# Feed-forward weights sized in the first sizing pass and turned beside the output projection

## The chip, the cores and the metric

One core of one Trainium2 chip runs the whole decoder layer as one program. The metric is the device time of that program in microseconds (us). TensorE (PE) multiplies, VectorE (DVE), ScalarE (ACT) and GpSimd (POOL) work elementwise, SyncE (SP) issues most DMAs. All of them run their own instruction streams and meet only at semaphores.

## What is computed

The layer is self-attention with 8-bit fake quantisation, cross-attention, and a feed-forward network, each with a residual and a layer norm behind it. Eight batches of 512 tokens of width 512. What matters for this change is the last part, and the projection in front of it:

```python
def fake_quant_weight(w, bits=8):
    scale = jnp.max(jnp.abs(w)) / 127
    return jnp.clip(jnp.round(w / scale), -128, 127) * scale
def qat_lora_linear(x, W, b, A, B):
    base = einsum('bsi,oi->bso', x, fake_quant_weight(W)) + b
    return base + 2 * einsum('bsr,or->bso', einsum('bsi,ri->bsr', x, A), B)
x = layernorm(x + (attended @ Wo + bo))             # x2 below
h = gelu(qat_lora_linear(x, W_fc, b_fc, A_fc, B_fc))      # W_fc: 2048 x 512
x = layernorm(x + qat_lora_linear(h, W_proj, b_proj, A_proj, B_proj))  # W_proj: 512 x 2048
```

The scale of each feed-forward weight is a maximum over the whole tensor, so no element can be quantised before all have been seen once. The ranks A and B are 16 wide. TensorE needs the weights with the contracted index on the partitions, so both weights and all four rank matrices are turned (transposed) through TensorE and PSUM.

## The kernel before

The program is a row of stages. All five engines meet at a barrier between stages: `barrier` (L218) drains an engine, adds one to `phase_end` and waits until all five have done so; `STAGES` lists them. Each stage streams the eight batches through scratch tensors in HBM. `arena` is one on-chip buffer carved anew for each stage, and `bank` is PSUM, eight banks of 128 x 512 f32. The stages that matter, in order:

- **First sizing pass** (up to barrier 3): `qkv_size` (TensorE, L845 and L850) computes the QKV product in pairs of banks only to find its largest value; `size_qkv` (VectorE, amax at L1398) reduces each pair. Twelve pairs per batch, four pairs fit in PSUM (`qkv_red` starts at 4). In the middle of a batch VectorE quantises the next one's input (`quantise_h`, L1565 and L1569). SP's queue stores that input and loads one two batches ahead (L437, L433).
- **Score rows** (up to barrier 6): ends with VectorE waiting for ScalarE's last sums (L1260) in `keep_rows`.
- **Cross-attention** (up to barrier 10): 32 groups of four heads. TensorE does L997, L1005, L1013 and L1041; VectorE reduces and clips (L1785, L1811). The last group's values are stored by SP (L597).
- **Output projection** (barrier 10 to 11): `project_out` (L1092) does 32 units of four f32 matmuls (each is two records in the trace), one bank per unit, eight banks in turn. VectorE's `second_norm` adds the bias (L1866), adds a bank to the residual (L1870), takes statistics (L1455), does a Newton square root (L1461 to L1472) and scales (L1480). SP stores the result, x2, to scratch and loads the next inputs (L675, L632, L629). ScalarE only issues the DMAs of the two weights (L1359), 4 MB each.
- **Weights** (barrier 11 to 12): for W_fc and then W_proj VectorE takes the maximum over 128 x 8192 (L1398), GpSimd reduces over partitions (L736), VectorE makes the scale, the int8 weight (L1918), the f16 weight (L1920), and spreads B (L1925). TensorE turns four 128 x 128 pieces into a bank (L1111), VectorE moves each bank out (L1896, and L1907 with L1908 for the A matrices, which are kept as an f16 and a remainder), and makes the remainder of B (L1947, L1950).
- **Feed-forward** (barrier 12 to 13): x2 of batch 0 is loaded back (L710), turned by TensorE (`turn_x2`, L1142), moved by ScalarE (L1369), split by VectorE (`split_x2`, L1959 and L1960), and `ranks` (L1149) multiplies it with A. Then `ffn` runs 16 slices per batch (L1162, L1165, L1173 to L1176) with ScalarE's Gelu (L1376) and VectorE's split (L1986, L1987). The norm of a batch is done in slices 1 to 3 of the next (`third_norm`).

The order of work on each engine is the order of the program; no planner is used.

## Time and profile before

| | us |
|---|---|
| three runs | 3144.04, 3149.09, 3150.22 (median 3149.09) |
| the profiled execution | 3145.82 |
| its span, first to last instruction | 3144.0 |
| TensorE / VectorE / ScalarE busy | 2659.6 / 2504.7 / 1443.7 |
| mean granted TensorE clock | 0.895 of full |

The page divides the span into 40 slices of 78.6 us. A digit is the busy share of the slice in tenths; `PEclk` is the clock that TensorE was granted, in tenths of 2.4 GHz, so 5 is 1.2 GHz. The profiled execution lies 3.3 us below the median of the runs.

### The profile page before, as it was taken

The numbers are of one execution on the slowest core, as the hardware profiler recorded it, in microseconds if no ns is written. First come the engines' busy times: TensorE is split into PE (matmuls) and PEld (weight loads), VectorE is DVE, ScalarE is ACT, GpSimd is POOL, SyncE is SP. The second block draws the span as 40 slices with busy tenths as digits, with TensorE's granted clock in tenths as the row PEclk, the third lists the DMA queues.
The fourth block names the chain that finished last, engine by engine and source line by source line (L and its number), as shares of the span: only waits on it lengthen the run. The fifth ranks groups of instructions, "written<-read, shape, count | busy, mean of one in ns | idle before, by whom it ended". The sixth has DMA issues, their size and how long they took to land. (4 is left out here: it accounts for less than half of the span.)

```text
span 3144.0 us, 44439 instructions
## 1 busy us (share of the span) xinstructions
PE 2659.6 (85%) x13112; PEld 1034.6 (33%) x13160; DVE 2504.7 (80%) x4278; ACT 1443.7 (46%) x2366; POOL 159.0 (5%) x147
## 2 busy tenths in 40 slices
PE   7999999967777747777769699999999379999997
PEld 4444432211111124444335222222224234444443
DVE  5988679999998979999888688888868854444454
ACT  3320043318999989999423255555530011211111
POOL 0000043310000000000000000111100000000000
PEclk9999999975555569999989899999999679999999
DMA  8561122214333333333125433434356200000000
GB/s 314 167 224 64 40 97 94 93 80 141 127 120 122 111 103 116 104 116 104 57 71 184 114 106 99 115 98 116 114 182 248 69 27 27 28 27 27 27 27 27
DMA packets 196495, 324.41 MB, mean 103 GB/s; under 512 B 32281, under 2 KB 118297, under 8 KB 187025
## 3 DMA queue, kind: packets, MB, share of 16 engines
q1 hardware_dynamic: 192160, 306.12, 30.0%
q10 hardware_dynamic: 4208, 16.78, 1.4%
q8 instruction: 58, 0.95, 0.1%
q14 instruction: 69, 0.56, 0.1%
HBM read 192.32 MB, written 130.51 MB: 103 GB/s over the span
## 5 line engine op out<-in xcount | busy, mean ns | idle before, releaser
L1398 DVE TENSOR_REDUCE stats<-bank 128x1024 f32 (+1 forms) x352 | 408.0, 1217 | 60.5 <-PE bank L845 28.1
L1260 ACT ACTIVATE arena<-arena,scale 128x512 bf16<-128x512 int8 x512 | 408.1, 799 | 53.4 <-DVE arena L1638 53.4
L905 PE MATMUL bank<-arena 64*128 64x512 bf16 x512 | 306.4, 605 | 104.9 <-DVE arena L1631 66.9
L1278 ACT ACTIVATE arena<-arena,scale 128x512 f32<-128x512 int8 x512 | 370.5, 803 | 13.1 <-DMA arena<-dq_scr 11.0
L1631 DVE CUSTOM_DVE_ANT_0 arena<-bank,arena,fac 128x512 int8<-128x512 f32 x512 | 349.8, 747 | 23.2 <-PE bank L905 10.2
L1785 DVE TENSOR_REDUCE arena<-bank 128x2 f32<-128x1024 f32 x256 | 312.5, 1223 | 54.7 <-PE bank L997 38.8
L1342 ACT ACTIVATE arena<-bank 128x1024 f32<-128x1024 f32 x256 | 248.0, 1022 | 189.4 <-PE bank L1013 189.4
L1376 ACT ACTIVATE arena<-bank,arena,fac 128x512 f32<-128x512 f32 x128 | 99.5, 777 | 458.8 <-PE bank L1165 458.8
L1041 PE MATMUL bank<-arena 128*32 128x512 f32 x2048 | 270.9, 606 | 0.0
L1248 ACT ACTIVATE arena<-bank,floor_c,fac 128x1024 int8<-128x1024 f32 x96 | 115.6, 1205 | 337.8 <-PE bank L845 287.2
L1986 DVE TENSOR_SCALAR arena<-arena 128x512 f16<-128x512 f32 x128 | 54.7, 428 | 260.7 <-ACT arena L1376 260.7
L845 PE MATMUL bank<-arena 128*128 128x512 bf16 x989 | 239.9, 382 | 11.3 <-DMA arena<-hq_scr 7.4
L1173 PE MATMUL bank<-arena 128*128 128x512 f16 x1024 | 242.0, 379 | 3.6 <-DVE arena L1987 3.2
L1162 PE MATMUL bank<-arena 128*128 128x512 f16 x1024 | 241.9, 379 | 0.0
L922 PE MATMUL bank<-identb,arena 128*128 128x128 bf16 x2048 | 138.8, 222 | 115.1 <-DVE arena L1684 115.1
L997 PE MATMUL bank<-arena 128*128 128x512 f16 x512 | 156.4, 389 | 25.1 <-DMA arena<-half_scr 13.0
L1811 DVE TENSOR_SCALAR arena<-arena 128x1024 f32<-128x1024 f32 (+1 forms) x192 | 168.2, 876 | 8.3 <-ACT arena L1342 8.3
L922 PEld LDWEIGHTS bank<-identb,arena 128*128 128x128 bf16 x2048 | 116.7, 99 | 176.6 <-DVE arena L1684 133.9
L1684 DVE TENSOR_SCALAR arena<-arena,inv 128x2048 bf16<-128x2048 f32 x128 | 163.5, 1277 | 10.8 <-ACT arena L1278 10.8
L905 PEld LDWEIGHTS bank<-arena 64*128 64x128 bf16 x512 | 51.7, 101 | 359.6 <-DVE arena L1631 349.4
L1665 DVE TENSOR_SCALAR arena<-bank 128x2048 bf16<-128x2048 bf16 x128 | 155.8, 1217 | 0.0
L1005 PE MATMUL bank<-arena 128*128 128x512 f16 x512 | 153.6, 383 | 0.0
(202 smaller groups left out, 3477.5 us busy)
## 6 DMA issues: line engine op xcount, KB each, us to landing
dq_scr<-arena SPq DMA_DIRECT2D x128, 256.0 KB, 2.0
arena<-dq_scr SPq DMA_DIRECT2D x128, 256.0 KB, 2.7
arena<-half_scr SPq DMA_DIRECT2D x256, 128.0 KB, 2.8
qkv_scr<-arena SPq DMA_DIRECT2D x8, 3072.0 KB, 9.7
arena<-in_x SPq DMA_DIRECT2D x16, 1024.0 KB, 8.4
half_scr<-arena SPq DMA_DIRECT2D x32, 512.0 KB, 4.1
arena<-qkv_scr SPq DMA_DIRECT2D x128, 128.0 KB, 2.2
x_scr<-arena SPq DMA_DIRECT2D x16, 1024.0 KB, 4.5
```

The lines of the kernel that those rows point to most:

```text
L845: last = mm(dst, wqkv_q[:, k, P * u:P * u + P], hq[:, k, :], start=k == 0, stop=k == KC - 1)
L905: return mm(dst, qE[r, h // 2, P * t:P * t + P], kE[r, h // 2, :], start=True, stop=True)
L922: last = nc.tensor.transpose(PT[s % 2][:, j, P * t:P * t + P], aG[:, s % 2, t, P * j:P * j + P], identb[:, :])
L1041: last = mm(bank[XD * g:XD * g + XD, 7 if k < 2 else 6, :], w, eT[:, par, g, c, :], start=c == 0, stop=c == NT - 1)
L1162: mm(dst, Wf[:, k, P * s:P * s + P], xx[:, par, k, :], start=k == 0 and n == 0, stop=False)
L1173: mm(bank[:, t, :], gg[:, f % 3, P * t:P * t + P], Wp[:, f, :], start=f == 0 and n == 0, stop=False)
L1260: last = A(e_dump[:, NT * (h % 2) + t, :], dq8[:, h % 4, t, :], ACT.Exp, bias=negm_b[:, par, c:c + 1], scale=scale[:, S_DOTS:S_DOTS + 1], ...
L1278: A(eG[:, s % 2, t, :], dqG[:, s % 4, t, :], ACT.Exp, bias=negm_g[:, par, c:c + 1], scale=scale[:, S_DOTS:S_DOTS + 1]).then_inc(S("eG_done ...
L1342: A(eT[:, r % 2, 2 * a:2 * a + 2, c, :], bank[:, 2 + 2 * a:4 + 2 * a, :], ACT.Exp, scale=XSCALE / HALF ** 2).then_inc(S("eX_done"), 1)
L1398: return V.tensor_reduce(dst, src, ax, ALU.max, apply_absolute_value=True)
L1631: V.tensor_tensor_reduce(dq8[:, s, t, :], bank[:, 4 * (h % 2) + t, :], floor_row, fac[:, C_DOTS:C_DOTS + 1], -3.0e38, ALU.add, ALU.max, ac ...
L1785: V.tensor_reduce(mxX[:, mp, hs, 2 * u:2 * u + 2], bank[:, at:at + 2, :], AX.X, ALU.max).then_inc(S("sX_red"), 1)
```

## The change

- **Sizing.** Both weights are read once more, in eight parts of 1 MB (128 x 2048 f32), during the first sizing pass. SP issues `load_part(0)` behind the first store of that pass and `load_part(b + 1)` behind `load_h(b + 2)`, each after a wait for the part before. VectorE reduces part b to `w_peak` behind pair 2 of batch b. The reduction to two peaks, GpSimd's reduction over partitions and four small scale steps go into the score-row stage.
- **Ranks.** The 16 DMAs of A and the two of B are issued by SP at the start of cross-attention; VectorE spreads B (`spread_ranks`, 16 instructions without a wait between them) in the last group.
- **Quantising.** ScalarE loads W_fc in four quarters behind its last cross-attention copy, makes it int8 in four passes of 128 x 2048 (`quantise_weight`), loads W_proj over it, widens W_fc to f16 in four passes (`widen_weight`), quantises W_proj, moves ten B copies, widens W_proj, and moves 32 weight banks.
- **Turning.** The projection uses banks 0 to 4 in turn and turns go to banks 5 to 7. TensorE turns the ten rank banks behind units 4 to 13, 16 banks of W_fc behind units 14 to 21, 16 of W_proj behind 22 to 29, and the first x2 behind 30 and 31. VectorE moves the five A banks in `halves_of_a` and subtracts the B halves in `halves_of_b` behind batch 4.
- **Barriers and order.** The diff takes 10, 11 and 12 out of `STAGES` and out of all engines. The norm of the last projected batch moves into slices 1 to 3 of the first feed-forward batch. SP's load of x2 for batch 0 now stands ahead of the last two stores of x2. The bias DMAs stand behind a wait for unit 3.
- Semaphore names `y_peak` and `o8_done` are replaced by ones in use; this changes no instruction's place.

```diff
-STAGES = (3, 5, 6, 7, 8, 9, 10, 11, 12, 13)
+STAGES = (3, 5, 6, 7, 8, 9, 13)
@@ first sizing pass, SP and VectorE
             for b in range(NB):
                 store_hq(b)
+                if b == 0:
+                    load_part(0)
                 if b + 2 < NB:
                     load_h(b + 2)
+                if b + 1 < NB:
+                    sp.wait_ge(S("part_in"), 16 * b + 16)
+                    load_part(b + 1)
...
+                    if u == 2:
+                        dve.wait_ge(S("part_in"), b * 16 + 16)
+                        amax(w_peak[:, bass.ds(b, 1)], part).then_inc(S("part_sized"), 1)
@@ cross-attention, SP and VectorE
+            for r in range(P // R):
+                sp.dma_start(arep_f[R * r:R * r + R, :], A_fc).then_inc(S("ranks_in"), 16)
+                sp.dma_start(arep_p[R * r:R * r + R, :], A_proj).then_inc(S("ranks_in"), 16)
...
+                        if last and (c, u) == (1, 0):
+                            spread_ranks()
@@ output projection, TensorE
-                    pe.wait_ge(S("wo_evac"), b * NT + t + 1)
+                if u >= 5:
+                    pe.wait_ge(S("wo_evac"), u - 4)
...
+            for u in range(NB * NT):
+                project_out(u // NT, u % NT)
+                if u == 4:
+                    pe.wait_ge(S("sumS_done"), GROUPS)
+                    pe.wait_ge(S("oX_evac"), GROUPS)
+                if 4 <= u < 14:
+                    turn_ranks(u - 4)
+                for n in (2 * u, 2 * u + 1):
+                    if 28 <= n < 44:
+                        turn_fc(n - 28)
+                    if 44 <= n < 60:
+                        turn_proj(n - 44)
+                    if 60 <= n:
+                        turn_first_x2(n - 60)
@@ output projection, ScalarE
+            for q in range(KC):
+                load_weight(wn[...], chunk(W_fc)[...], q)
+            quantise_weight(0, S_WFC)
+            for q in range(KC):
+                act.wait_ge(S("w8_done"), q + 1)
+                load_weight(wn[...], chunk(W_proj)[:, q, :], q)
+            widen_weight(wnh)
+            quantise_weight(1, S_WPROJ)
+            for n in range(5):
+                moved_by_act(half, 5 + n)
+                moved_by_act(full, 5 + n).then_inc(S("w_moved_act"), 1)
+            act.wait_ge(S("w8_done"), 8)
+            widen_weight(wnp)
+            for n in range(FC):
+                moved_by_act(Wf[...], 10 + n, True).then_inc(S("w_moved_act"), 1)
+            for n in range(FC):
+                moved_by_act(Wp[:, n, :], 26 + n, True).then_inc(S("w_moved_act"), 1)
@@ output projection, VectorE
+            for b in range(NB - 1):
+                ch = add_projected(b)
+                for k in range(3):
+                    second_norm(ch, b, k)
+                ch.end()
+                if b == 4:
+                    halves_of_b()
+            add_projected(NB - 1)
```

A turn beyond the third waits for the move of the turn three before it (`MOVED_BY`): five moves by VectorE, then 37 by ScalarE, then ScalarE's copies of x2.

## Rows read from the trace of the kernel before

**Rows 1.** The page: granted TensorE clock by slice of 78.6 us.
```profile
PEclk9999999975555569999989899999999679999999
```
**Rows 2.** TensorE's waits, 2330 to 2560 us: waiter, cause, total, times, longest.
```profile
PE bank L1111 <- DVE arena L1920: 58.2, 2, 31.4
PE bank L1142 <- DMA arena<-x_scr: 9.9, 1, 9.9
PE bank L1092 <- POOLq L220: 6.2, 1, 6.2
```
**Rows 3.** Timeline, 2296 to 2360 us: start, duration, instruction, idle before it.
```profile
2326.56 7.93 PE L1041 MATMUL bank<-arena 128*32 128x512 f32 x72
...
2340.72 19.82 PE L1092 MATMUL bank<-arena 128*128 128x512 f32 x39 [6.23 <-POOLq L220]
```
**Rows 4.** Timeline, 2536 to 2610 us: the first x2, the first ranks, a later x2.
```profile
2550.41 0.43 DVE L1959 CAST arena<-arena 128x512 f16<-128x512 f32 x1 [0.65 <-ACT arena L1369]
2550.87 0.69 DVE L1960 TENSOR_TENSOR arena<-arena 128x512 f16<-128x512 f32 x1
...
2551.62 3.38 PE L1149 MATMUL bank<-arena 128*128 128x512 f16 x8 [1.88 <-DVE arena L1960]
...
2585.78 0.60 PE L1142 MATMUL bank<-ident,arena 128*128 128x128 f32 x4
...
2586.21 1.89 PE L1162 MATMUL bank<-arena 128*128 128x512 f16 x8
```
**Rows 5.** Busy time by stretch: length, PE, PEld, DVE, ACT, POOL, PEclk, DMA share, GB/s.
```profile
2341.00:2344.00 3.00, 3.00 (x4) 1.23 (x5) 2.12 (x4) 0.00 (x0) 0.00 (x0) 0.50 0.76 206
...
2352.00:2400.00 48.00, 48.00 (x113) 21.22 (x112) 37.06 (x99) 0.00 (x0) 0.00 (x0) 1.00 0.73 282
...
2520.00:2532.00 12.00, 8.34 (x76) 8.08 (x77) 11.56 (x26) 0.00 (x0) 0.00 (x0) 0.55 0.00 0
```
**Rows 6.** Groups by line and shape, 2462 to 2538 us: busy, mean ns, idle before.
```profile
L1398 DVE TENSOR_REDUCE peak<-arena 128x1 f32<-128x8192 f32 x2 | 17.4, 8686 | 4.0 <-ACTq L220 4.0
L1918 DVE TENSOR_SCALAR arena<-arena,fac 128x8192 int8<-128x8192 f32 x2 | 9.0, 4486 | 0.1
L1950 DVE TENSOR_TENSOR arena<-arena 32x2048 f16<-32x2048 f32 x2 | 4.6, 2284 | 0.1
...
L1907 DVE TENSOR_SCALAR arena<-bank 128x512 f16<-128x512 f32 x5 | 3.4, 683 | 0.0
```
**Rows 7.** Timeline of the weights stage: turns of f16 pieces, four to a bank.
```profile
2525.55 5.30 PE L1111 MATMUL bank<-identh,arena 128*128 128x128 f16 x48 [0.87 <-DVE arena L1896]
```
**Rows 8.** ScalarE by size: groups of the page, one of 150 to 400 us.
```profile
L1278 ACT ACTIVATE arena<-arena,scale 128x512 f32<-128x512 int8 x512 | 370.5, 803 | 13.1 <-DMA arena<-dq_scr 11.0
L1376 ACT ACTIVATE arena<-bank,arena,fac 128x512 f32<-128x512 f32 x128 | 99.5, 777 | 458.8 <-PE bank L1165 458.8
L1248 ACT ACTIVATE arena<-bank,floor_c,fac 128x1024 int8<-128x1024 f32 x6 | 7.2, 1206 | 180.1 <-PE bank L845 180.1
```
**Rows 9.** Groups by line and shape, 2352 to 2452 us: VectorE's cycle of a batch.
```profile
L1870 DVE TENSOR_TENSOR arena<-bank,arena 128x512 f32<-128x512 f32 x29 | 18.7, 687 | 13.6 <-PE bank L1092 12.6
```
**Rows 10.** Timeline of the first sizing pass, 196 to 262 us.
```profile
216.75 0.96 SPq L437 DMA_DIRECT2D hq_scr<-arena  x1
...
219.21 1.23 DVE L1398 TENSOR_REDUCE stats<-bank 128x1 f32<-128x1024 f32 x1 [0.50 <-PE bank L845]
...
227.26 1.27 DVE L1565 TENSOR_SCALAR arena<-arena,inv 128x2048 int8<-128x2048 f32 x1
```
**Rows 11.** Groups, 150 to 400 us: a reduction of a whole 128x2048 tile.
```profile
L1398 DVE TENSOR_REDUCE stats<-arena 128x1 f32<-128x2048 f32 x3 | 6.8, 2281 | 0.3 <-ACT arena L1208 0.3
```
**Rows 12.** DMA issues, 2330 to 2400 us: KB each, us to landing.
```profile
arena<-in_L_ffn_W_fc ACTq DMA_DIRECT2D x1, 4096.0 KB, 15.0
```
**Rows 13.** Timeline, 1120 to 1140 us: VectorE at the end of the score rows.
```profile
1128.75 0.20 DVE L1619 COPY neg_m<-arena 128x64 f32<-128x64 f32 x1 [9.29 <-ACT arena L1260]
```
**Rows 14.** Timeline, 2296 to 2350 us: VectorE in the last cross-attention group.
```profile
2322.41 1.23 DVE L1811 TENSOR_SCALAR arena<-arena 128x2048 f32<-128x2048 f32 x1 [2.52 <-ACT arena L1342]
```

More of the change, by code:

```diff
@@ L683, in after_batch @@
                 load_x1(b + 2, par)
+            sp.wait_ge(S("wo_mm"), NT)
+            with nc.allow_non_contiguous_dma(reason="a column of 2048 numbers"):
+                sp.dma_start(bf_s[:, :], col(b_fc)).then_inc(const_in, 16)
+            sp.dma_start(bp_s, b_proj.rearrange("(a n) -> a n", a=1).broadcast_to([P, D])).then_inc(const_in, 16)
             with sp.Fori(0, NB // 2 - 1) as j:
@@ new lines, in project_out @@
+            def project_out(b, t):
+                u = b * NT + t
+                if t == 0:
+                    pe.wait_ge(S(f"oK_in{b % 2}"), 16 * (b // 2) + 16)
+                if u >= 5:
+                    pe.wait_ge(S("wo_evac"), u - 4)
+                for o in range(KC):
+                    last = mm(bank[:, u % 5, :], oK[:, b % 2, o, P * t:P * t + P], Wo_s[:, o, :],
+                              start=o == 0, stop=o == KC - 1)
+                last.then_inc(S("wo_mm"), 1)
+            turned = [0]
@@ new lines, in weight_bank, with turn_f32 @@
+            def weight_bank():
+                n = turned[0]
+                turned[0] += 1
+                if n >= 3:
+                    engine, count = MOVED_BY[n - 3]
+                    pe.wait_ge(S(engine), count)
+                return bank[:, 5 + n % 3, :]
+            def turn_f32(parts):
+                dst = weight_bank()
+                for q, src in enumerate(parts):
+                    last = nc.tensor.transpose(dst[:, P * q:P * q + P], src, ident[:, :])
+                last.then_inc(S("w_turned"), 1)
@@ new lines, in widen_weight, with moved_by_act @@
+            def widen_weight(dst):
+                for q in range(4):
+                    r = slice(QW * q, QW * q + QW)
+                    A(dst[:, r], wn8[:, r], ACT.Copy).then_inc(S("wnh_ready"), 1)
+            def moved_by_act(dst, n, f16=False):
+                act.wait_ge(S("w_turned"), n + 1)
+                src = bank[:, 5 + n % 3, :]
+                return A(dst, src.bitcast(F16)[:, 0:512] if f16 else src, ACT.Copy)
+            for q in range(KC):
+                load_weight(wn[:, QW * q:QW * q + QW].rearrange("p (a d) -> p a d", d=D), chunk(W_fc)[:, KC * q:KC * q + KC, :], q)
@@ L1873, in second_norm @@
-                norm_stats(ch, xK[:, par])
-                for t in range(NT):
-                    last = normed(xK[:, par, t, :], xK[:, par, t, :], t)
-                last.then_inc(S("x2_ready"), 1)
-                ch.end()
-            batches(dve, second_norm)
-            barrier(dve, 11)
-            pair = ((S_WFC, C_FC, B_FCS, 9), (S_WPROJ, C_PROJ, B_PROJS, 10))
-            moved = [0]
-            def move(dst, src_rows=slice(0, P), cast=None, scale_by=None):
-                n = moved[0]
-                moved[0] += 1
-                dve.wait_ge(S("w_turned"), n + 1)
-                src = bank[src_rows, n % 4, :]
-                if cast:
-                    src = src.bitcast(F16)[:, 0:512]
-                if len(dst.shape) == 3:
-                    src = src.rearrange("p (a b) -> p a b", b=P)
-                if scale_by is None:
-                    return V.tensor_copy(dst, src)
-                return V.tensor_scalar(dst, src, scale_by, None, ALU.mult)
@@ new lines, in add_projected, with second_norm @@
+                    if 4 <= u < 9:
+                        halves_of_a(u - 4)
+                return ch
+            def second_norm(ch, b, k):
+                par = b % 2
+                if k == 0:
+                    dve.wait_ge(S("wo_evac"), b * NT + NT)
+                    norm_moments(ch, xK[:, par])
+                if k == 1:
+                    norm_factors(ch)
+                if k == 2:
+                    for t in range(NT):
+                        last = normed(xK[:, par, t, :], xK[:, par, t, :], t)
+                    last.then_inc(S("x2_ready"), 1)
```

296 lines of the change are left out of this document (144 added, 152 removed).

## The prediction

> **What bounds the kernel now.** I read the slices first, then TensorE's waits, then the timeline around them. The granted clock falls to 7 and 9 tenths in two neighbouring slices near the end [rows 1]; these slices hold the weights stage. TensorE's waits there name the reason: 58.2 us in two waits for VectorE's f16 weight, 9.9 us for the first x2 to come back, 6.2 us at the barrier behind cross-attention [rows 2]. The timeline gives the two ends. The last cross-attention matmul ends at 2334.5 us (2326.56 + 7.93) and the first matmul of `ranks` starts at 2551.6 [rows 3, 4]. Everything that the change moves at the end of the kernel lies in these 217.1 us. In them TensorE needs its time only for the projection: inside a full-clock stretch one record takes 48/112 = 0.43 us [rows 5] (113 are listed, one cut at the edge), so 256 records need 109.7 us. The rest, 107 us, is barriers, half clock and VectorE's serial chain on the weights. Behind it the feed-forward is all TensorE, and in front of it cross-attention isn't touched. So the question is how much of 107 us comes back.
>
> **The new path, part by part.** I lay out TensorE's stream from 2334.5 us on.
>
> - *Barrier behind cross-attention gone.* Its 6.2 us [rows 2] go. TensorE's own conditions (output of the reductions, the first inputs) are long met; banks 0 to 3 were read before the last clip. Because TensorE doesn't pause, the half clock behind the pause goes too: 39 records took 19.8 us where 39 x 0.43 is 16.7 [rows 3], and the row from 2341 shows 0.50 [rows 5]. Both are contained in counting the projection at 109.7 us straight from 2334.5.
> - *Turns of ranks.* Ten banks of f32. A bank costs TensorE 0.43 us at full clock: a turned x2 bank starts at 2585.78 and the next work at 2586.21 [rows 4]. 10 x 0.43 = 4.3 us.
> - *Turns of weights.* 32 banks of f16. In the weights stage 48 pieces, twelve banks, took 5.3 us [rows 7], 0.44 us a bank, at a clock of about 0.55 [rows 5]. At 1.2 GHz that is 0.44, at 2.4 GHz half of it. Bounds 7 and 14 us; I take 7, since the stretch from 2352 to 2400 shows 1.00 with nothing but this matmul [rows 5] and the turns add to TensorE's work. These are 6.7 us at 0.21.
> - *First x2.* Two of its four banks behind unit 30: 0.9 us. The other two lie in the drain below.
> - *Waits for the moves.* A turn waits for the move three before it. ScalarE moves the last B bank just behind unit 13, two copies of at most 0.78 us [rows 8], and then widens W_proj, four passes of 128 x 2048, before the first W_fc bank can be moved. The trace has no pass of that size. ScalarE's rows give 0.78 us for 512 and 1.21 for 1024 elements, 0.84 ns an element [rows 8], so 2.07 us for 2048. From above it can't exceed four passes of 512 with an SBUF source, 4 x 0.80 = 3.2 us [rows 8]. With 2.07 the first W_fc bank is free 1.5 + 8.3 + 0.7 = 10.5 us behind unit 13, while TensorE wants it after two units and three turns, 7.5 us. Stall 3.0 us; 7.5 with 3.2 us a pass; none if the passes start early. I take 3.0, from the rows with a like size step. Later turns come two to a unit of 3.43 us and find their banks moved.
> - *PSUM.* The projection has five banks instead of eight. VectorE needs 13.7 - 1.9 = 11.8 us a batch (13.6 us idle over 29 adds, four to a batch) [rows 9]. From the add of a batch's last bank to the first of the next lie about 11 us, with the B halves (2 x 2.3 us and two small ones, some 6 us [rows 6]) 17 us. The unit that reuses that bank starts five units and their turns later, over 18 us. No stall, margin 1 to 2 us. The A halves (0.68 + 0.42 us each, five [rows 6]) fall in batches 1 and 2, where the ten rank turns give VectorE 0.43 us a unit more; it ends 1 us behind and catches up.
> - *DMAs.* W_fc landed 15.0 us after its issue while W_proj was in flight beside it [rows 12]. Now W_fc goes at 2335, W_proj at about 2352, behind the fourth int8 pass; widening W_fc covers its landing. W_proj is int8 by about 2370, and the first B bank is turned at 2371. SP issues the two bias DMAs ahead of the inputs of batch 2, which then leave at 2351 for use at 2364; an input of this size is in flight with W_proj, 5 MB at the stretch's 282 GB/s [rows 5], so at the worst 18 us if all of W_proj went first. I cost it at nothing, and 5 us if it did.
> - *The drain.* Behind unit 31 VectorE adds the last bank (0.2 + 0.69 us [rows 9]), then splits four pieces of x2, 0.43 + 0.69 us each with no wait on ScalarE any more [rows 4], 4.6 us with gaps; then `ranks`. 5.6 us. The norm of batch 7 is no longer here. It goes beside slices 1 to 3 of the first feed-forward batch, where the norm of the batch before stands in every other batch.
>
> Sum: 109.7 + 4.3 + 6.7 + 0.9 + 3.0 + 5.6 = 130.2 us against 217.1, a gain of 86.9 us. I leave `ranks` at its old 3.38 us (half clock [rows 4]), since TensorE idles nearly 5 us ahead of it and 6.2 us of idle was enough for 0.50 [rows 3, 5].
>
> *What is paid elsewhere.* (1) First sizing pass: a pair costs TensorE 1.73 us and VectorE 1.23 with 0.50 idle [rows 10]. Twelve pairs leave 6 us, `quantise_h` takes 2.5 of them (1.27 and a like cast [rows 10]); the new reduction takes 2.28 [rows 11]. So it fits: the lag behind pair 2 is mostly made up before `quantise_h` and never reaches 3.9 us, what four pairs in PSUM allow. Batch 0 is different. Its part is issued at 217.7 behind the store [rows 10], and VectorE wants it at 220.4. I take 8 us to land, half of what 4 MB beside another 4 MB took [rows 12]: 1 MB, but behind stores and a load in the same queue. Landing at 225.6 makes pair 3 free at 229.1 instead of by 226.1: 3.0 us (0 for a landing before 222.5, 6 for 228.5). If VectorE's new work hid behind nothing it would be 8 x 2.28 = 18.3 us. (2) Score rows: one tiny reduction in front, 0.3 us; the four scale steps at the end stand before a copy that waited 9.29 us for ScalarE [rows 13]: nothing. (3) Spreading B: 16 small instructions, about 5 us, ahead of two clips that waited 2.5 and 1.9 us in the last group [rows 14], with more idle behind; I cost it at 0, at most 1. (4) 18 DMA issues at the start of cross-attention: SP there waits for the end of group 0 anyway: 0.
>
> 3145.8 - 86.9 + 3.0 + 0.3 = 3062.2 us. The profiled execution lies 3.3 us below the median of runs, which spread over 6 us; I add nothing for that.
>
> *A rule that speaks against the change.* VectorE made an int8 weight at 4486/8192 = 0.55 ns an element [rows 6], ScalarE's rows give 0.84 [rows 8]. The Trainium skill (ScalarE: Activation LUTs, Rules for kernel authors) says to use VectorE and not ScalarE for such plain arithmetic, VectorE being up to about three times faster an element. The trace agrees in direction, at 1.5 times. By three times, a pass of 2048 would be about 3.4 us as an estimate from that page, the stall above some 8 us and the time about 3067.
>
> **The rivals.**
>
> *A. ScalarE sets the pace.* The 16 large passes cost 3.2 us each [rows 8]. For it: no such pass is in the trace, and ScalarE did nothing here before. Against: the step from 512 to 1024. Stall 7.5 instead of 3.0: 3066.7; with inputs of batch 2 late as well, 3072.
>
> *B. The reductions aren't hidden in the sizing pass.* For it: VectorE is TensorE's partner at every pair there. Against: it idles 0.50 us at each pair [rows 10]. 18.3 instead of 3.0 us: 3077.5.
>
> *C. The first x2 isn't early.* SP loads it behind a store and a load of batch 5; if it is only issued when unit 31 ends, the 9.9 us that TensorE waits for it now [rows 2] come back: 3072. Against: it should leave four units before it is wanted.
>
> *D. Clock and landing are kind.* TensorE keeps 2.4 GHz through the drain (`ranks` in 1.7 instead of 3.38 us), part 0 lands in time and ScalarE is early: 3062.2 - 1.7 - 3.0 - 3.0 = 3054.5.
>
> *E. Slower: half clock in the projection.* If the many waits on moves made TensorE's projection run at 1.2 GHz, its 121.6 us of work would take 243.2: 3184, slower. The gain of 83.6 is used up when 83.6/121.6, 69%, of that stretch is at half clock. For it: 0.50 follows a pause of 6.2 us [rows 3, 5]. Against: between full-clock matmuls of 3.43 us a unit there is one expected wait of 3 us in 125. The Trainium skill (TensorE: Matmul & The Clock Gate, A second HAM failure mode) describes a kernel whose cycling through PSUM banks let the clock swing between both levels; no row here shows it for such short gaps.
>
> *F. It doesn't do what it says*: a wait I have overlooked holds the turns until the projection is over. 42 banks at ScalarE's 0.78 us each plus the passes, some 45 us back: 3107.
>
> **How the numbers follow.** Forecast 0.66, A 0.13, B 0.07, C 0.02, D 0.08, E 0.02, F 0.02. The range runs from D's 3054, less 1, to B's 3077, plus 3: 3053 to 3080; it leaves out E, F and the tails. A measurement of this kernel can tell about 0.2%, 6.3 us, from no change. All cases but E are faster by more than that; I give faster 0.96, same 0.01, slower 0.03.
>
> **What the profile will show.** Right: TensorE passes from L1041's successor to the projection without a pause and at 1.00; one stall of 2 to 4 us behind unit 15, waiting for ScalarE; ScalarE's 2048 passes near 2.1 us; `ranks` about 130 us behind the last cross-attention matmul; sizing pass longer by 3 us in batch 0 and by nothing later; the feed-forward as long as now. Wrong: TensorE waits in several units for ScalarE or DMA, a PEclk under 0.9 in the projection, or a longer stretch between units 19 and 24, where VectorE subtracts the B halves.

## The result: 3063.8 us where 3062.2 was forecast

| | before | after |
|---|---|---|
| median of four runs, us | 3146.95 (3144.04 to 3150.22) | 3063.81 (3063.38 to 3064.36) |
| profiled execution / its span | 3145.82 / 3144.0 | 3064.36 / 3062.6 |
| TensorE / VectorE / ScalarE busy | 2659.6 / 2504.7 / 1443.7 | 2652.0 / 2462.7 / 1495.8 |
| granted TensorE clock | 0.895 | 0.905 |

After to before is 0.9736, 95% interval 0.9719 to 0.9752: 83 us less. The sum was 1.6 us off the median and 2.2 us off the profiled execution. That closeness is partly luck: the late inputs of batch 2 cost 4.2 us that the sum didn't have, while the stall for ScalarE was 1.7 us shorter and the stretch from `ranks` to the end 1.9 us shorter than in it. Line numbers have moved: the projection is now L1111, ranks L1200, the last cross-attention matmul L1057, the reductions (amax) L1486, the split of x2 L2031 and L2032.

The slices of the page of after, to be held against [rows 1]:

```profile
PE   7999989986777747777678889999999999999997
...
PEclk9999999995555559999988989999999999999999
```

The low slices at the weights stage are gone. Counted along the row they are slices 32 and 33 of [rows 1], at 6 and 7 tenths of full clock; the prediction read 7 and 9, which enters no sum. What TensorE still waits for between 2330 and 2500 us in after (waited for, us in total, times, longest), where [rows 2] had 58.2, 9.9 and 6.2:

```profile
PE bank L1200 <- DVE arena L2032: 4.2, 1, 4.2
PE bank L1111 <- DMA arena<-oT_scr: 2.4, 1, 2.4
PE bank L1135 <- ACT arena L1426: 1.3, 1, 1.3
```

The first is the drain, foreseen. The third is the stall for ScalarE, 1.3 us where I had 3.0. The second I had costed at nothing. TensorE's timeline of after shows all three in place (start us, us, engine, line, operands, count, idle before and what ended it), with the projection's first record right behind the last cross-attention record (2329.91 + 7.93):

```profile
2329.91 7.93 PE L1057 MATMUL bank<-arena 128*32 128x512 f32 x72
2337.78 4.56 PE L1111 MATMUL bank<-arena 128*128 128x512 f32 x10
...
2366.66 0.60 PE L1129 MATMUL bank<-ident,arena 128*128 128x128 f32 x4
2369.65 5.40 PE L1111 MATMUL bank<-arena 128*128 128x512 f32 x8 [2.39 <-DMA arena<-oT_scr]
...
2402.06 0.39 PE L1135 MATMUL bank<-identh,arena 128*128 128x128 f16 x4
2403.70 0.40 PE L1135 MATMUL bank<-identh,arena 128*128 128x128 f16 x4 [1.26 <-ACT arena L1426]
...
2458.59 0.61 PE L1135 MATMUL bank<-identh,arena 128*128 128x128 f16 x8
2459.04 3.65 PE L1111 MATMUL bank<-arena 128*128 128x512 f32 x8
2462.53 1.04 PE L1167 MATMUL bank<-ident,arena 128*128 128x128 f32 x8
2463.40 3.60 PE L1111 MATMUL bank<-arena 128*128 128x512 f32 x8
2466.84 1.04 PE L1167 MATMUL bank<-ident,arena 128*128 128x128 f32 x8
2472.12 2.72 PE L1200 MATMUL bank<-arena 128*128 128x512 f16 x8 [4.25 <-DVE arena L2032]
```

The stretch from the last cross-attention matmul to `ranks` is 2472.12 - 2337.78 = 134.3 us. It was 217.1 before, and 130.2 in the forecast.

**The whole account of the profiled execution.** Up to the end of cross-attention after is 3.3 us later (2337.8 against 2334.5; forecast 3.3). The projection stretch is 82.8 us shorter (forecast 86.9). From `ranks` to the end it takes 590.5 instead of 592.4 us (forecast: the same). Then 3.3 - 82.8 - 1.9 = -81.4, and 3145.8 - 81.4 = 3064.4, what was measured.

### The profile page after: what moved, and what is told of

It reads as the page before. It is cut to its first block, busy times and chain, and to the rows that moved or that the text cites. A ratio compares the mean times of both kernels' runs of the same rounds, so it can differ in the third digit from the quotient of the medians.

```text
span 3062.6 us, 44241 instructions
## 1 busy us (share of the span) xinstructions
PE 2652.0 (87%) x13112; PEld 1025.9 (33%) x13160; DVE 2462.7 (80%) x4238; ACT 1495.8 (49%) x2424; POOL 159.1 (5%) x146
## 4 chain that ended last, share of the span: by engine, by line
PE 50%; issue 30%; DVE 15%; ACT 2%; DMA 1%; DVEq 1%; SPq 0%; ACTq 0%; POOLq 0%; POOL 0%
PE bank L1057 8%; PE bank L1224 7%; PE bank L1213 7%; DVE stats L1486 6%; PE bank L1013 4%; PE bank L1021 4%; PE bank L997 4%; PE bank L1111 3%; DVE arena L1785 2%; PE bank L834 1%; PE bank L841 1%; PE bank L1029 1%; ACT arena L1329 1%; PE bank L972 1%; PE bank L861 1%
## 5 line engine op out<-in xcount | busy, mean ns | idle before, releaser
L1486 DVE TENSOR_REDUCE stats<-bank 128x1024 f32 (+1 forms) x352 | 405.9, 1215 | 44.1 <-PE bank L898 26.8
L1329 ACT ACTIVATE arena<-arena,scale 128x512 f32<-128x512 int8 x512 | 370.3, 802 | 13.3 <-DMA arena<-dq_scr 11.3
L1462 ACT ACTIVATE arena<-bank,bf_s,fac 128x512 f32<-128x512 f32 x128 | 99.5, 778 | 459.2 <-PE bank L1216 459.2
L1057 PE MATMUL bank<-arena 128*32 128x512 f32 x2048 | 270.1, 604 | 0.0
L861 PE MATMUL bank<-arena 128*128 128x512 bf16 x989 | 240.3, 383 | 14.3 <-DMA arena<-hq_scr 7.4
```

The source lines that it names most:

```text
L861: last = mm(dst, wqkv_q[:, k, P * u:P * u + P], hq[:, k, :], start=k == 0, stop=k == KC - 1)
L1057: last = mm(bank[XD * g:XD * g + XD, 7 if k < 2 else 6, :], w, eT[:, par, g, c, :], start=c == 0, stop=c == NT - 1)
L1329: A(eG[:, s % 2, t, :], dqG[:, s % 4, t, :], ACT.Exp, bias=negm_g[:, par, c:c + 1], scale=scale[:, S_DOTS:S_DOTS + 1]).then_inc(S("eG_done ...
L1486: return V.tensor_reduce(dst, src, ax, ALU.max, apply_absolute_value=True)
```

## The experiments

All ran in rounds beside the kernel before. Totals of one kernel spread over 1 to 7 us, so effects of a few us are read from local stretches of the traces, and totals only where they are larger. For all of them, T is the time from the start of the projection to the start of `ranks`.

| kernel | median, us | ratio to before, 95% | T, us | wait for batch 2's inputs, us |
|---|---|---|---|---|
| after | 3063.81 | 0.9736 (0.9719 to 0.9752) | 134.3 | 2.4, then half clock |
| after_again | 3065.22 | 0.9751 (0.9734 to 0.9767) | 132.7 | 2.4 |
| e_bias_late | 3062.01 | 0.9739 (0.9723 to 0.9755) | 130.0 | none |
| e_wproj_wait | 3060.90 | 0.9736 (0.9720 to 0.9753) | 130.0 | none |
| e_part0_early | 3061.22 | 0.9732 (0.9715 to 0.9748) | 134.4 | 2.4, then half clock |
| e_widen_early | 3063.63 | 0.9742 (0.9726 to 0.9759) | 130.8 | 2.0 |
| e_x2_late | 3063.83 | 0.9745 (0.9729 to 0.9762) | 132.2 | 2.2 |
| e_splits_all | 3059.15 | 0.9732 (0.9716 to 0.9748) | 128.8 | 2.2 |
| e_turns_twice | 3072.90 | 0.9772 (0.9756 to 0.9788) | 140.6 | 2.2, then half clock |
| e_barrier10 | 3068.01 | 0.9754 (0.9737 to 0.9770) | 133.1 | 0.6 |
| e_reduce_twice | 3067.05 | 0.9750 (0.9734 to 0.9766) | 136.2 | 2.9, then half clock |
| e_reduce_thrice | 3091.11 | 0.9828 (0.9812 to 0.9845) | 133.1 | 2.9 |
| e_best | 3047.55 | 0.9693 (0.9677 to 0.9710) | 124.9 | none |

after_again is the changed kernel once more. It ran beside the first three experiments; the local stretches of the others are held against it too.

> The changed kernel once more, unedited, as the yardstick on this chip for the three runs beside it. Both theories: 3063 to 3065 us, span about 3062.6, TensorE idle 2.4 us for the values of batch 2 and 2.85 us in the first sizing pass.

The 2.4 us wait came back, the half clock behind it didn't: the next eight records took 3.70 instead of 5.40 us. The granted clock of 2370 to 2374 us, first in after, then in after_again (stretch, length, busy us and count by engine, clock, DMA share, GB/s):

```profile
2370.00:2374.00 4.00, 4.00 (x7) 1.51 (x6) 3.37 (x17) 0.00 (x0) 0.00 (x0) 0.58 0.46 166
```

```profile
2370.00:2374.00 4.00, 4.00 (x13) 1.91 (x12) 3.31 (x18) 0.00 (x0) 0.00 (x0) 1.00 0.43 139
```

So 1.7 us of after's 134.3 differ between executions of one program.

### Why batch 2's inputs were late

In after SP issued two bias loads at 2351.87 and 2352.30, and the values of batch 2 at 2353.94. The bias of W_fc is a column of 2048 four-byte pieces. The four W_proj loads of 1 MB left ScalarE's queue at the same time. The line that loads the values, and their time to landing, in after:

```profile
L649 SPq DMA_DIRECT2D arena<-oT_scr x8: 383/392/441, 2278.4 to 2435.4; - x8
...
DMA to landing us min/median/max: 5.4/6.6/15.7
```

The median load lands in 6.6 us, this one in 15.7. Two edits separate the two neighbours. The first moves the bias loads behind the inputs of batches 2 to 7:

```diff
-            sp.dma_start(bf_s[:, :], col(b_fc)).then_inc(const_in, 16)
-            sp.dma_start(bp_s, b_proj.rearrange("(a n) -> a n", a=1).broadcast_to([P, D])).then_inc(const_in, 16)
             with sp.Fori(0, NB // 2 - 1) as j:
                 after_batch(j * 2, 0)
                 after_batch(j * 2 + 1, 1)
+            sp.dma_start(bf_s[:, :], col(b_fc)).then_inc(const_in, 16)
+            sp.dma_start(bp_s, b_proj.rearrange("(a n) -> a n", a=1).broadcast_to([P, D])).then_inc(const_in, 16)
```

> The two bias DMAs are issued behind the loop over the batches instead of ahead of it. Theory (the values of batch 2 come late because SP's queue first issues and moves the biases, 2048 pieces of 4 bytes and a broadcast): they leave 2 us earlier and land before unit 8; the wait of 2.4 us and the half clock behind it (8 records in 5.4 instead of 3.6 us) go, 4.2 us less than the unedited kernel, about 3059.8. Rival (the 4 MB of W_proj in flight at once are what slows them): they leave 2 us earlier and land at most 2 us earlier, 0 to 2 us less, and the half clock may stay.

The wait is gone and T is 130.0 us. The values landed 13.6 us after their issue, 1.2 us before TensorE came for them. The second edit leaves the biases and holds ScalarE's four loads of W_proj until the values are in:

```diff
+            act.wait_ge(S("oK_in0"), 32)
             for q in range(KC):
                 act.wait_ge(S("w8_done"), q + 1)
                 load_weight(wn[:, QW * q:QW * q + QW], chunk(W_proj)[:, q, :], q)
```

> ScalarE waits for the values of batch 2 to have landed before it issues the four loads of W_proj; the biases stay where they are. Theory of the bias DMAs: the values land hardly earlier, no change beyond 1 us. Rival (W_proj's traffic): the values land at about 2361 instead of 2369.6, the 2.4 us wait and the half clock go, 4.2 us less; W_proj is then int8 at about 2379 instead of 2370, still before ScalarE is wanted for the B banks, so nothing is given back. About 3059.8.

The values landed in 6.2 us, ScalarE stood 8.0 us for them, the wait of TensorE is gone, and T is again 130.0 us. The issues of this kernel and their landing show the biases freed as well: 3.0 us for `bf_s`, where after had 11.3, and 4.3 for `bp_s`, where after had 14.3 (what is loaded, queue, count, KB, us to landing).

```profile
arena<-in_L_ffn_b_proj SPq DMA_DIRECT2D x1, 256.0 KB, 4.3
...
bf_s<-in_L_ffn_b_fc SPq DMA_DIRECT2D x1, 8.0 KB, 3.0
```

It isn't the 2048 pieces that hold the values up, though. In e_x2_late and e_turns_twice, which leave both biases and W_proj as in after, `bf_s` landed in 3.0 us too, and the values still took 15.6. How late `bf_s` lands goes with its lead over the first load of W_proj: 3.0 us at leads of 0.77 and 0.68 us, 6.2 to 7.1 at 0.63 and 0.62, 11.3 to 13.5 at 0.55 to 0.51 (after, after_again, e_part0_early), while the values took 15.3 to 15.9 in all seven.

So the wait needs both: W_proj's 4 MB are the larger part (15.7 to 6.2). The two biases together are some 3.6 us: without them the values leave some 1.5 us earlier, counted from the start of the projection, and fly 2.1 us less. Which of the two biases matters, no run separates. Either edit is enough to end the wait. Both edits leave T at 130.0 us: everything in my sum but this one term adds up to the 130.2 I had, in part because the f16 turns (1.4 us over) and the stall for ScalarE (1.7 under) cancel. T falls by 2.7 us against after_again; the totals fall by 3.2 and 4.3, no more than their spread.

### The first part of W_fc

```diff
                         load_h(n)
+                    sp.dma_start(w_parts[:, 0, :], W_fc.rearrange("(p a) d -> p (a d)", p=P)[:, 0:KC * D]
+                                 ).then_inc(S("part_in"), 16)
                 sp.wait_ge(S("v_ready"), b * NT + NT)
...
-                if b == 0:
-                    load_part(0)
```

> Part 0 of W_fc is loaded behind the first two loads of the quantised input's source, some 18 us earlier. Theory (the only price of the sizing pass is VectorE waiting 5.0 us for part 0, of which TensorE's four pairs of banks hide all but 2.85): those 2.85 us go and every later part stays hidden, about 3061. Rival (the reduction itself costs, wherever its data is): TensorE still waits in the sizing pass, less than 1 us gained. Third: the load now collides with the input load that VectorE waits 6.6 us for, and 1 to 3 us are lost there instead.

The timeline of after, at the place of [rows 10]: VectorE stands 5.02 us for the part, and TensorE in its turn 2.85 us for VectorE. First VectorE, then TensorE:

```profile
225.41 2.29 DVE L1486 TENSOR_REDUCE w_peak<-arena 128x1 f32<-128x2048 f32 x1 [5.02 <-DMA arena<-in_L_ffn_W_fc]
227.62 4.61 DVE L1486 TENSOR_REDUCE stats<-bank 128x1 f32<-128x1024 f32 x4
```

```profile
214.00 12.03 PE L861 MATMUL bank<-arena 128*128 128x512 bf16 x54 [1.40 <-ACT arena L1280]
228.89 1.90 PE L861 MATMUL bank<-arena 128*128 128x512 bf16 x8 [2.85 <-DVE stats L1486]
```

With the load ahead of the wait both waits are gone. L866 of batch 0 starts at 227.55 us, where the kernel before has 227.64 and after 230.63, and the projection starts at 2335.0, where the eight kernels with this stretch unedited and no barrier in front start at 2337.0 to 2339.6. The term of 3.0 us is shown, and so is its cause. What the wait costs later varies: in seven of the other kernels half clock follows it.

### How much of VectorE is free in the sizing pass

Rival B said the reductions would not hide. In after they do: eight batches of the first sizing pass follow each other at 20.7 us as before (L866 starts at 230.63, 251.42, ... 375.74; in the kernel before at 227.64, 248.36, ... 372.68). Reducing each part twice (one added line) or three times (both) finds the edge.

```diff
+                        amax(tmpf[:, 6:7], part)
+                        amax(tmpf[:, 7:8], part)
                         amax(w_peak[:, bass.ds(b, 1)], part).then_inc(S("part_sized"), 1)
```

> In the first sizing pass VectorE reduces each part of W_fc twice (2.2 us more a batch), to measure how much of VectorE's time is really free there. Worked out: a batch costs TensorE 20.7 us (12 pairs of 1.73), VectorE 12 x 1.16 + 2.19 + 2.5 = 18.6 us back to back, so 2.1 us are free. Theory (the free time decides, four pairs in PSUM even it out): the second reduction just about fits, 0 to 4 us for the eight batches, all in all, beside the 2.2 us that batch 0 pays, since its part lands late: total 2 to 6 us up. Rival (lags behind a pair aren't made up before the quantising and each batch pays): 2.2 x 8 = 17 us.

> The same with each part reduced three times (4.4 us more a batch). Theory: VectorE then needs 23.0 us a batch against TensorE's 20.7 and sets the pace: 2.3 us for each of eight batches, 18 us, and some 2 us for batch 0: total 15 to 22 us up, and the free time comes out as 4.4 us less the lengthening of a batch. Rival (every reduction is paid in full): 35 us. Rival (the free time is larger than worked out): under 10 us.

Twice: 147.5 us from the first to the eighth L866 instead of 145.1. Of these 2.4 us 1.0 lies in the first batch, which still has half clock behind its wait (32 records in 8.00 us, 7.14 in after), and 0.2 to 0.3 in each other one, without a wait of TensorE. Its one large wait, in batch 0, is 5.0 instead of 2.9 us. The total is in the 2 to 6 us of the theory; the projection starts at 2343.7, 4 to 7 us later than elsewhere. Three times: TensorE waits for VectorE in every batch, and the seven batches take 166.7 us, 3.1 a batch where 2.3 was expected; the total is up by some 26 us, above the 15 to 22 I gave. TensorE's waits in the first sizing pass of e_reduce_thrice:

```profile
PE bank L861 <- DVE stats L1486: 22.9, 8, 7.7
```

Of them 7.7 us are batch 0's, and the other seven are 2.1 to 2.2 us each, as the theory has it. The size was off because of what follows the wait. TensorE's timeline, two batches in a row:

```profile
280.30 1.90 PE L861 MATMUL bank<-arena 128*128 128x512 bf16 x8 [2.22 <-DVE stats L1486]
282.04 7.14 PE L866 MATMUL bank<-arena 128*128 128x512 bf16 x32
...
303.49 3.29 PE L861 MATMUL bank<-arena 128*128 128x512 bf16 x8 [2.22 <-DVE stats L1486]
306.57 7.41 PE L866 MATMUL bank<-arena 128*128 128x512 bf16 x32
```

In four of the seven batches the eight records behind the wait take 1.90 us and the batch is 23.0 to 23.5 us long. In the other three they take 3.3 to 3.5 us (granted clock 0.57 from 303.4 to 306.6 us, 1.00 from 328.3 to 330.0) and the batch is 24.5 to 24.7. So the lengthening is 2.5 us a batch at full clock, and half clock in three batches adds 4.3 us in all. Batch 0 adds 5.2 (its L866 starts at 235.84, in after at 230.63) where some 2 were expected. VectorE itself still stands now and then, 6.9 us in all from 240 to 400 us, in the pairs ahead of each burst:

```profile
317.57 1.23 DVE L1486 TENSOR_REDUCE stats<-bank 128x1024 f32 x1 [0.50 <-PE bank L861]
319.29 1.22 DVE L1486 TENSOR_REDUCE stats<-bank 128x1024 f32 x1 [0.50 <-PE bank L861]
320.44 4.47 DVE L1486 TENSOR_REDUCE tmpf<-arena 128x1 f32 x2
324.82 2.28 DVE L1486 TENSOR_REDUCE w_peak<-arena  x1
```

So 4.4 - 2.5 = 1.9 us a batch are free, where 2.1 had been worked out, and the second reduction takes 2.2 of them for 0.2 to 0.3. The change's own 2.2 us a batch is hidden in full, with some 2 us of room behind it.

### What a turn costs

```diff
                 dst = weight_bank().bitcast(F16)
                 for q, src in enumerate(parts):
+                    nc.tensor.transpose(dst[:, P * q:P * q + P], src, identh[:, :])
+                for q, src in enumerate(parts):
                     last = nc.tensor.transpose(dst[:, P * q:P * q + P], src, identh[:, :])
```

> Each of the 32 f16 weight banks is turned twice by TensorE (the same four transposes again into the same bank), so that their cost appears a second time. Theory (turns lie on TensorE's path at their full price and the moves behind them are hidden): a unit with two turns goes from 3.93 to 4.35 to 4.45 us, the stretch from the last cross-attention matmul to ranks from 134.3 to 141 to 142.5 us, the total 7 to 8 us up. Rival 1 (turns hide under the weight loads or in waits for ScalarE): under 2 us. Rival 2 (ScalarE or VectorE sets the pace of these units, and turns only wait): under 2 us and TensorE's waits for ScalarE shrink instead.

In after a unit with two f16 banks takes 3.93 us, with them 0.45 and the unit 3.49, since the matmuls behind a turn run 3.65 instead of 3.60 us:

```profile
2434.98 0.61 PE L1135 MATMUL bank<-identh,arena 128*128 128x128 f16 x8
2435.43 3.65 PE L1111 MATMUL bank<-arena 128*128 128x512 f32 x8
2438.91 0.61 PE L1135 MATMUL bank<-identh,arena 128*128 128x128 f16 x8
```

Doubled (L1135 and the new L1137), a unit takes 4.38 us, 2430.57 to 2434.95:

```profile
2430.57 0.39 PE L1135 MATMUL bank<-identh,arena 128*128 128x128 f16 x4
2430.79 0.39 PE L1137 MATMUL bank<-identh,arena 128*128 128x128 f16 x4
2431.01 0.39 PE L1135 MATMUL bank<-identh,arena 128*128 128x128 f16 x4
2431.24 0.39 PE L1137 MATMUL bank<-identh,arena 128*128 128x128 f16 x4
2431.46 3.65 PE L1111 MATMUL bank<-arena 128*128 128x512 f32 x8
2434.95 0.39 PE L1135 MATMUL bank<-identh,arena 128*128 128x128 f16 x4
```

That is 0.22 us a bank, on the path in full: T is 140.6, and less the 1.6 us of half clock that this execution has and after_again doesn't (5.34 for 3.70), 138.9. Against after_again's 132.7 it is 6.3 us, plus 0.7 that the stall for ScalarE shrank (1.3 to 0.6) and 0.2 that the input wait did: 7.2 for 32 banks. The total is up by some 8 us over after_again. Rival F, turns that wait, would have shown waits for ScalarE at every unit; there is one.

### ScalarE's order

The four passes that widen W_proj go ahead of the ten moves of B instead of behind them:

```diff
+            act.wait_ge(S("w8_done"), 8)
+            widen_weight(wnp)
             for n in range(5):
                 ...
                 moved_by_act(full, 5 + n).then_inc(S("w_moved_act"), 1)
-            act.wait_ge(S("w8_done"), 8)
-            widen_weight(wnp)
```

> ScalarE widens W_proj to f16 (four passes of 1.83 us) right behind its last int8 pass, ahead of the moves of the five B banks, and no longer behind them. In the changed kernel ScalarE idles 9.5 us there, and TensorE later waits 1.3 us for the first W_fc bank to be moved. Theory (the wait is only the order on ScalarE): the int8 passes end near 2370, widening near 2377, the first B bank is turned at 2378; so the 1.3 us wait is gone, no other takes its place, and the stretch from the last cross-attention matmul to ranks goes from 134.3 to 133.0 us. In the total that is 1.3 us, below what totals can tell. Rival (ScalarE has no slack before the B banks, its passes end when W_proj lands): the B moves come late by as much as the landing is late, and a wait of 1 to 5 us appears at the rank turns.

T is 130.8 us with an input wait of 2.0; after_again less its 1.3 us stall and 0.4 of input wait would be 131.0. The stall is gone and nothing took its place. ScalarE's timeline of after shows the 9.49 us that stood free ahead of the B moves, and its passes:

```profile
2354.88 7.31 ACT L1421 ACTIVATE arena<-arena 128x2048 f16<-128x2048 int8 x4 [0.47 <-ACT arena L1416]
2362.22 7.68 ACT L1416 ACTIVATE arena<-arena,inv 128x2048 int8<-128x2048 f32 x4
2379.40 1.08 ACT L1426 ACTIVATE arena<-bank 128x512 f16<-128x512 f32 x2 [9.49 <-PE bank L1129]
```

### The drain

e_x2_late turns all four pieces behind the last unit:

```diff
-                    if 60 <= n:
-                        turn_first_x2(n - 60)
+            for k in range(KC):
+                turn_first_x2(k)
```

> All four pieces of the first x2 are turned behind the last projection unit, none behind the one before. Theory (the drain between the last unit and ranks is VectorE's: last add, then four splits of 1.03 us; TensorE idles 4.2 us in it): unit 31 ends 0.9 us earlier, the drain is 5.6 to 5.8 instead of 5.3 us, since piece 0 is copied by ScalarE only 1.1 us behind the unit; from the last cross-attention matmul to ranks 133.6 to 133.9 instead of 134.3 us. Rival (turning two pieces early is what keeps the drain short): 135.5 us or more, drain 7 us.

The drain is 5.9 us (2463.25 to 2469.14) instead of 5.3, the unit before it 0.9 us earlier, and T is 132.2 against 132.7 (0.2 of it is the input wait): turning two pieces early is worth nothing, it costs 0.3 us, as long as VectorE only begins to split when the last bank has been added. e_splits_all turns all four behind unit 30 and lets VectorE split them while it would wait for unit 31:

```diff
                     u = b * NT + t
+                    if u == NB * NT - 1:
+                        dve.wait_ge(const_in, 16 * 5)
+                        for k in (0, 1, 2, 3):
+                            split_x2(first, 0, 0, k)
                     dve.wait_ge(S("wo_mm"), u + 1)
@@ TensorE
-                    if 60 <= n:
-                        turn_first_x2(n - 60)
+                if u == NB * NT - 2:
+                    for k in range(KC):
+                        turn_first_x2(k)
```

> All four pieces of the first x2 are turned behind unit 30, and VectorE splits all four in f16 pairs before it adds the last projected bank; it idles 3.6 us there in the changed kernel. Theory (the drain is VectorE's serial work of 5.1 us behind the last unit): splits end near the end of unit 31, ranks starts under 1 us behind it, at full clock: the drain goes from 5.3 to about 1 us, and the 0.9 us of two more turns ahead of unit 31 take the place of the same two behind it; from the last cross-attention matmul to ranks some 131 instead of 134.3 us (129.9 to 131.5), and ranks 1.7 to 1.9 instead of 2.7 us: 4 to 5 us in the total. Rival (it comes back later, the norm of batch 7 and the last add then meet the first feed-forward slices, or TensorE waits for VectorE in slice 0): the stretch is shorter, the total within 1 us.

TensorE's timeline of e_splits_all:

```profile
2462.27 2.00 PE L1167 MATMUL bank<-ident,arena 128*128 128x128 f32 x16
2464.11 3.60 PE L1111 MATMUL bank<-arena 128*128 128x512 f32 x8
2468.15 1.89 PE L1201 MATMUL bank<-arena 128*128 128x512 f16 x8 [0.45 <-DVE arena L2027]
```

`ranks` starts 0.45 us behind unit 31 and runs at full clock (1.89 us; 2.72 in after, and 2.5 to 3.6 us in the other kernels whose TensorE idled 3.9 to 4.3 us ahead of it). T falls by 3.9 us against after_again, 3.7 with equal input waits, and from `ranks` to the end it takes 588.8 us where after and after_again both have 590.5. Nothing came back later: the rival is refuted by the profile. The median is 4.7 us below after's and 6.1 below after_again's, but the kernel's own four runs spread over 7.2 us and its interval overlaps both, so here too the gain rests on the profiles.

### The barrier

```diff
-STAGES = (3, 5, 6, 7, 8, 9, 13)
+STAGES = (3, 5, 6, 7, 8, 9, 10, 13)
@@ TensorE, and likewise each other engine, behind its cross-attention
+            barrier(pe, 10)
```

> The barrier between cross-attention and the projection is put back (all engines wait for each other there); everything else stays as in the changed kernel. Theory (the barrier costs its wait and the half clock behind it, as in the kernel before): TensorE waits 6.2 us, the projection then starts at half clock as before (39 records in 19.8 instead of 16.7 us), so some 9 us from the last cross-attention matmul to ranks; the output-projection inputs and the weight loads also leave later, and the wait for the inputs of batch 2 moves with them: 134.3 becomes 141 to 144 us, the total 3070 to 3073. Rival (the barrier is covered, since the loads of W_fc and ScalarE's passes are the longest chain): under 3 us, or above 12 us if the chain of ScalarE, which starts only behind the barrier, then sets the pace of the turns.

TensorE's timeline of e_barrier10:

```profile
2345.16 19.66 PE L1114 MATMUL bank<-arena 128*128 128x512 f32 x40 [6.08 <-SPq L221]
...
2377.45 3.70 PE L1114 MATMUL bank<-arena 128*128 128x512 f32 x8 [0.57 <-DMA arena<-oT_scr]
```

It has the barrier's 6.1 us and the half clock behind it: 40 records in 19.66 us, where e_best needs 17.43 for 40. That is 8.3 us, near the theory's 9. But from the last cross-attention matmul to `ranks` it took 139.1 us, 6.4 more than after_again and not the 141 to 144 I expected, and the total is some 3 to 4 us up instead of 6 to 9. The input wait shrank from 2.4 to 0.6 us, which is nearly all of the 1.9 us between 8.3 and 6.4. Counted from the start of the projection, the values left 8.0 us later than in after_again (23.9 against 16.0) and yet landed at the same point, 32 us behind it; TensorE came for them 2.2 us later, by its half clock. So it is the half clock behind the barrier that covers part of the wait; the barrier's own pause moved the loads of the weights with it. Why the totals show still less than the trace stays open; their spread is 3 us on either side.

### All four together

e_best joins e_part0_early, e_bias_late, e_widen_early and e_splits_all.

> Four edits together: part 0 of W_fc is loaded ahead of the wait and the last stores of the step before, the two bias loads follow the inputs of batches 2 to 7, ScalarE widens W_proj right behind its int8 passes, and all four pieces of the first x2 are turned behind unit 30 and split ahead of the last add. Theory (each removes its own wait and they add up): no wait for weights in the sizing pass (3 us), none for the inputs of batch 2 (2.2 to 4.2 us), none for ScalarE (1.3 us), drain near 1 instead of 5.3 us with ranks at full clock (4 to 5 us): from the last cross-attention matmul to ranks 125 to 126 instead of 134.3 us, from ranks to the end 588.8, total 3050 to 3054 us. Rival (they lean on the same slack: with biases later W_proj or ScalarE's widening is late and the B banks wait): above 3056 us.

TensorE's waits in e_best between 2320 and 2500 us, of which one is left:

```profile
PE bank L1201 <- DVE arena L2027: 0.4, 1, 0.4
```

T is 124.9 us, `ranks` to the end 588.8. The median is 3047.55 us (3046.76 to 3051.34), 0.9693 of before (0.9677 to 0.9710), an interval that doesn't touch that of after. That is below the 3050 to 3054 expected. Between the spans of after_again and e_best lie 15.6 us: 7.8 in T, 1.7 behind it, 4.2 up to the start of cross-attention (3.8 in e_part0_early alone), and 1.9 in cross-attention itself (572.0 us from its first record to the projection, 573.9 in after_again), which no edit touches. The last I don't count as won: 572.0 is the lowest of all fourteen profiles, which reach up to 576.2. T agrees with what the edits did alone (2.7 + 1.3 + 3.7 = 7.7), and so do the other two, so they add up.

## Why the prediction was right, point by point

- **No pause into the projection, full clock, 0.43 us a record.** Right. Cross-attention's last record meets the projection's first, and e_barrier10 brings back 6.1 + 2.2 us where 6.2 + 3.1 had been read from the rows; the half clock was shorter there.
- **Turns.** Ranks 0.44 us a bank: right. f16 banks: 8.1 us (0.50 a unit of two banks, 16 units) where I had 6.7. The transposes themselves cost 0.22 to 0.23 a bank where 0.21 was taken, 7.2 us; the other 0.9 us is that the eight f32 records behind them take 3.65 instead of 3.60 us, which the prediction left out.
- **ScalarE.** The int8 pass was 2.00 us (2.07 by the row with the like size step), but the widening pass only 1.83, and a move 0.54 instead of 0.7: stall 1.3 instead of 3.0. Rival A, 3.2 us a pass, is out. The Trainium skill (ScalarE: Activation LUTs, Rules for kernel authors) would have such arithmetic on VectorE, up to about three times faster in bf16; the prediction left that condition out and used the figure for f32 to int8. For that the rows give 2.00 us against 0.55 x 2048 = 1.13 us, 1.8 times, and not the 3.4 us a pass of its estimate. But ScalarE's 30 us of passes are off the path but for 1.3 us, and e_widen_early removes even these by order alone.
- **DMAs.** The step that failed, a wait put at nothing. I named the inputs of batch 2, gave the worst case (18 us) and the price (5 us), and then took nothing. They landed in 15.7 us where 13.3 would have done (issued at 2353.94, wanted at 2367.3), which cost 2.4 us in both executions of the changed kernel, and 1.8 us of half clock in one (5.40 us for eight records that take 3.60 in an unbroken run). The 4.2 us of after are nearly the whole miss of T (134.3 against 130.2); e_bias_late and e_wproj_wait show T = 130.0 without it. The reasoning that W_fc landed in 15.0 us beside W_proj [rows 12] was at hand and should have been used for this load too.
- **The drain.** 5.3 us where I had 5.6, and made of VectorE's serial work, as e_x2_late and e_splits_all show. The 0.9 us for two early turns bought nothing.
- **`ranks` and the end.** I left it at 592.4 us and it was 590.5. 0.7 is `ranks` itself (2.72 for 3.38). TensorE's waits for L1987 [after: L2057] fell from 3.2 to 1.1 us; the largest of before, 2.6 us near 2848, lay behind a pause of 1.86 us of VectorE for which the trace names only issue. That neither I nor any run explains. It offset half of the DMA term.
- **Sizing.** 3.0 forecast; the part landed 7.9 us after its issue at 217.52, where I had 8, and the stretch is 3.0 us later at batch 0's end. The room left beside it is some 1.9 us a batch; the prediction's figures (6 less 2.5 less 2.28) gave 1.2. So rival B is out, by less than one more reduction.
- **Score rows, spreading B, DMA issues.** The score rows start 3.4 us late and end 4.2 us late (1112.6 to 1116.8): up to 0.8 us where 0.3 was given. The other two show no wait.
- **PSUM, rivals C and F.** TensorE's three waits shown above are all that it has from 2330 to 2500 us. So no unit waited for VectorE to free one of the five banks, also where the B halves are subtracted, the first x2 was there when it was wanted, and no turn was held back until the projection was over.
- **Rival D.** Two of its three kindnesses came in part: ScalarE was 1.7 us early, and `ranks` 0.7 us shorter though not at full clock. Part 0 was not in time.
- **Rival E, half clock.** Out of 126 us from 2338 to 2464 the clock was 0.99. The Trainium skill (TensorE: Matmul & The Clock Gate, A second HAM failure mode) tells of a kernel that swings while cycling through PSUM banks; here, with eight banks cycling and 42 turns between, only the 4 us behind the input wait were below full.

## What to carry to other kernels

When a large load is moved to another queue, list every transfer that then flies beside it and whose use is near; price the worst of them by the slowest landing in the trace, not by the median. A stage whose engines once met at a barrier has waits that the barrier covered: removing it can gain less than its own length, here 6.4 of 8.3 us by one trace. And at the end of a stage look for what the slower engine could do while it waits for the last unit: reordering VectorE's splits gave 3.7 us, more than turning data early did.

## What the runs showed of the hardware

- **Half clock behind a short pause is not certain.** A pause of 2.2 to 2.4 us in front of the same matmuls was followed by records at 5.3 to 5.4 us for eight in after, e_part0_early and e_turns_twice, and by 3.70 for eight in after_again (1.00 granted), e_x2_late and e_splits_all. In one execution of e_reduce_thrice it went both ways: behind seven waits of 2.1 to 2.2 us eight bf16 records took 1.90 us four times and 3.3 to 3.5 us three times. Behind the wait of 2.6 to 3.3 us in batch 0 of the sizing pass they took from 1.90 (after, after_again, e_x2_late, e_turns_twice) to 3.59 us (e_bias_late). Behind 3.9 to 4.3 us of idling the eight matmuls of `ranks` took anything from 2.47 to 3.57 us; at full clock it is 1.89.
- **A small load can be late by how closely a large one follows it.** 8 KB in 2048 pieces landed in 3.0 us with 4 MB leaving on another queue 0.68 us or more behind it, and in 11.3 us or more with the 4 MB 0.55 us or less behind. Why isn't shown. In e_barrier10, where the 4 MB left 2.7 us ahead of the pieces, SP needed 6.74 us to issue the broadcast bias that follows them, where it needed 1.17 in after, and from the issue of the pieces to that of the values it took 7.6 us for 2.1. That is one run.
- **Cross-attention alone, unedited, took 572.0 to 576.2 us** from its first record to the projection, or to the barrier in front of it, over all fourteen profiles. A cause wasn't looked for.
